# Metaformer block on one core: padded copies laid out by halves of rows, and half A's attention sums taken out of PSUM by ACT and added by Pool

## The reference

```
x = x + conv(layernorm(x))          # over the last axis
t = tokens(x)                       # (16, 1024, 32)
t = t + ffn(layernorm(t))

conv: q, k, v = Wq x, Wk x, Wv x    # 32 x 32 matrices over channels
  qk[n,i,h,j]  = sum_c q[n,c,i,j] k[n,c,h,j] / d
  qrq, krk     = sum_c q[n,c,i,j] rq[c,h,i] / d, the same with k and rk
  weight = softmax over j of (qk + Gq qrq + Gk krk)
  out[n,c,i,j] = sum_h weight[n,i,h,j] Gv1 v[n,c,h,j] + sum_h weight[n,i,h,j] Gv2 rv[c,h,i]
ffn: Wx = t W^T, batch-normed over all tokens, times gamma plus beta
  y_t = sigmoid(Wx_t + y_(t-1) V^T), y_0 = 0
```

## Time and profile before

| | us |
|---|---|
| median of 3 runs | 149.83 (149.29 to 151.29) |
| the profiled execution's own time | 149.44 |
| its span, first to last instruction | 147.7 |
| PE busy | 113.8 (77%) |
| DVE busy | 100.7 (68%) |
| ACT busy | 79.0 (53%) |
| Pool busy | 61.0 (41%) |

### The profile page before, as it was taken

The page is one execution under the profiler, slowest core; times in us unless marked ns, Lnnn a source line. Parts: engine busy times, 40 slices in busy tenths (PEclk is TensorE's granted clock), DMA queues, the critical chain, the costliest instruction groups (busy, mean ns, idle before and its releaser), DMA issues.

```text
span 147.7 us, 4779 instructions
## 1 busy us (share of the span) xinstructions
PE 113.8 (77%) x2102; PEld 80.9 (55%) x2102; DVE 100.7 (68%) x148; ACT 79.0 (53%) x146; POOL 61.0 (41%) x69
## 2 busy tenths in 40 slices
PE   0697995967899999991498598599994987999300
PEld 0322231667887668991498597544331336999300
DVE  5898646060300199789593079999879969788992
ACT  8958767704449997363620003506252459999400
POOL 8995919820000001978820033998052000004940
PEclk9999999999999999999559999999999999999985
DMA  4882640762000000009345200000000000000567
GB/s 142 288 230 37 142 107 0 177 178 83 4 4 4 0 0 4 4 4 208 81 101 129 63 4 7 7 0 0 4 0 0 0 0 0 4 0 0 168 191 209
DMA packets 8287, 9.55 MB, mean 65 GB/s; under 512 B 2316, under 2 KB 6412, under 8 KB 8268
## 3 DMA queue, kind: packets, MB, share of 16 engines
q1 hardware_dynamic: 8268, 9.26, 24.5%
HBM read 2.97 MB, written 2.10 MB: 34 GB/s over the span
## 4 chain that ended last, share of the span: by engine, by line
DVE 28%; PE 28%; ACT 19%; issue 10%; SPq 5%; DMA 4%; POOL 3%; ACTq 0%
PE ps L983 8%; ACT rel_tile L492 6%; PE ps L1019 6%; PE ps L998 5%; ACT warm L634 4%; DVE xin L345 3%; SPq L290 3%; DVE stat L671 3%; DVE u_tile L772 3%; PE ps L1031 3%; DVE y_tile L351 3%; DVE stat L785 3%; DMA xin<-in_x_dram 2%; PE ps L1007 2%; DVE rel_tile L803 2%
## 5 line engine op out<-in xcount | busy, mean ns | idle before, releaser
L401 POOL TENSOR_TENSOR att_tile<-att_tile,soft 128x1024 f32<-128x1024 f32 x4 | 7.8, 1955 | 28.8 <-DVE soft L732 28.8
L492 ACT COPY rel_tile<-ps 128x512 f32<-128x512 f32 x8 | 15.4, 1977 | 4.4 <-PE ps L998 4.3
L571 ACT ACTIVATE square<-y_tile 128x512 f32<-128x512 f32 x8 | 5.1, 640 | 22.6 <-POOL y_tile L422 19.9
L998 PE MATMUL ps<-spread,r_fac 128*32 128x128 f32 x256 | 16.3, 406 | 0.9 <-ACT rel_tile L492 0.7
L351 POOL TENSOR_TENSOR y_tile<-xin,u_tile 128x256 f32<-128x256 f32 (+1 forms) x7 | 7.1, 1048 | 23.5 <-DVE xin L345 23.5
L726 DVE TENSOR_TENSOR att_tile<-ps,rel_tile 128x1024 f32<-128x1024 f32 x4 | 8.3, 2063 | 12.5 <-ACT rel_tile L492 12.5
L1019 PE MATMUL ps<-spread,rv_t 128*32 128x128 f32 x256 | 11.4, 353 | 5.1 <-issue 5.1
L1091 PE MATMUL ps<-blank 128*128 128x512 bf16 x64 | 15.1, 379 | 0.0
L998 PEld LDWEIGHTS ps<-spread,r_fac 128*32 128x32 f32 x256 | 12.3, 126 | 4.5 <-ACT rel_tile L492 3.6
L983 PE MATMUL ps<-spread,u_tile 128*32 128x64 f32 x512 | 12.6, 253 | 2.6 <-issue 1.3
L983 PEld LDWEIGHTS ps<-spread,u_tile 128*32 128x32 f32 x512 | 12.2, 192 | 3.2 <-issue 3.0
(11 more groups left out here) (108 smaller groups left out, 227.2 us busy)
## 6 DMA issues: line engine op xcount, KB each, us to landing
spread<-rel_tile SPq DMA_DIRECT2D x16, 128.0 KB, 2.4
out_dram<-y_tile SPq DMA_DIRECT2D x8, 256.0 KB, 2.3
xin<-in_x_dram SPq DMA_DIRECT2D x3, 512.0 KB, 4.9
spread<-att_tile SPq DMA_DIRECT2D x12, 128.0 KB, 2.4
xin<-in_x_dram SPq DMA_DIRECT2D x2, 256.0 KB, 2.8
spread<-u_tile SPq DMA_DIRECT2D x4, 128.0 KB, 2.3
att_tile<-in_L_conv_rv_dram SPq DMA_DIRECT2D x4, 128.0 KB, 2.5
att_tile<-in_L_conv_rq_dram SPq DMA_DIRECT2D x1, 128.0 KB, 6.1
```

Of the source, the lines that this page charges most:

```text
L492: nc.scalar.copy(rel[:, n // 4, :, rows, :], side_bank(n).rearrange("p (i g j) -> p g i j", i=ROWS, g=G)).then_inc(S["rel_ready"], 1)
L998: ins = nc.tensor.matmul(side_bank(n)[group(q), P * k:P * (k + 1)].rearrange("p (g jp t) -> p g jp t", g=G, t=RUN), r_fac[:, ROWS * n + k, ...
```

## The change

Padded images are stored in halves of rows: `(b jp i t)`, with `b` the half and only 16 rows of pairs in each. The next pair of a row now lies 128 bytes on. The attention weights of half A go to the first 2 KB of each image, and those of half B to the second. `turn_y` on ACT therefore becomes two copies of 512 columns for each `q`, and each `weigh` two instructions, one for each image. The four images `g` of the weights now lie along the first axis of `spread4`, 16 KB apart; before, two were 16 KB apart and two lay 128 bytes apart. Half A's spread waits for `score_a` and the first four relative blocks in place of `score_b_high`. `weigh(1)` moves from Pool to DVE. Half A's weighted sums are copied out of PSUM by ACT (`sums_out`) and added to x2 by Pool (`sums_add`); DVE keeps the row sums. Unit 7's centring and scaling move from DVE to Pool, the last two `bn_part` read PSUM, and the orders are written anew.

```diff
-        y_bd = spread4[:, :, :, :].rearrange("p q g (jp i t) -> p q g jp i t", i=C, t=RUN)
-        att_bd = spread4[:, :, :, :].rearrange("p x q (jp g i t) -> p x q jp g i t", g=2, i=HALF, t=RUN)
+        y_bd = spread4[:, :, :, :].rearrange("p q g (b jp i t) -> p q g b jp i t", b=2, i=HALF, t=RUN)
+        att_bd = spread4[:, :, :, :].rearrange("p g q (b jp i t) -> p g q b jp i t", b=2, i=HALF, t=RUN)
...
             def spread_att(n):
                 wait_weights(sp, n)
-                sp.wait_ge(S["score_b_high"], 1)
+                half, gs = n // 2, slice(2 * (n % 2), 2 * (n % 2) + 2)
+                sp.wait_ge(S["score_b_high" if half else "score_a"], 1)
+                sp.wait_ge(S["rel_product"], PIECES4 // 2 * (half + 1))
                 for q in range(Q):
-                    sp.dma_start(spread4[group(q), n, q, :], rel_tile[group(q), IMG * n:IMG * (n + 1)]
-                                 ).then_inc(S[f"att_in{n // 2}"], 16)
+                    sp.dma_start(spread4[group(q), gs, q, BANK * half:BANK * (half + 1)],
+                                 rel_tile[group(q), IMG * n:IMG * (n + 1)].rearrange("p (g k) -> p g k", g=2)
+                                 ).then_inc(S[f"att_in{half}"], 16)
...
+            def sums_add(k):
+                pool.wait_ge(S["first_sums"], k + 1)
+                nc.gpsimd.tensor_tensor(unit(x2, k), first_sums[:, k, :, :], unit(x2, k), ALU.add).then_inc(S["x2_added"], 1)
...
-                nc.scalar.copy(in_pairs(turned_y[q]), by_pairs(y[:, q, :, :])).then_inc(S["y_turned_act"], 1)
+                for b in range(2):
+                    nc.scalar.copy(in_pairs(turned_y[q])[:, b], by_pairs(y[:, q, HALF * b:HALF * (b + 1), :])).then_inc(S["y_turned_act"], 1)
...
+            def sums_out(k):
+                act.wait_ge(S["wsum_product"], 1)
+                act.wait_ge(S["relv_ready"], 4)
+                nc.scalar.copy(first_sums[:, k, :, :], ps[:, 0:4, :].rearrange("p b (j q i) -> p q i (b j)", q=Q, i=HALF)[:, k]
+                               ).then_inc(S["first_sums"], 1)
...
-                                               r_fac[:, ROWS * n + k, :], y_bd[:, q, :, :, ROWS * n + k, :],
+                                               r_fac[:, ROWS * n + k, :], y_bd[:, q, :, n // 4, :, ROWS * (n % 4) + k, :],
...
-                                               rv_t[:, ROWS * n + k, :], att_bd[:, 2 * half + g // 2, :, :, g % 2, row + k, :],
+                                               rv_t[:, ROWS * n + k, :], att_bd[:, g, :, half, :, row + k, :],
...
-            pe.wait_ge(S["x2_ready"], Q)
-            blank_banks([0, 1] + [WARM_BANK] * 16)
-            for n in range(4):
-                project_wx(n)
-                blank_banks([WARM_BANK] * 4)
-            pe.wait_ge(S["x2_ready"], UNITS)
-            blank_banks([4, 5, 6, 7] + [WARM_BANK] * 10)
+            pe.wait_ge(S["x2_added"], Q)
+            blank_banks([0, 1] + [WARM_BANK] * 8)
+            project_wx(0)
+            blank_banks([WARM_BANK] * 4)
+            project_wx(1)
+            pe.wait_ge(S["x2_ready"], Q)
+            blank_banks([4, 5, 6, 7] + [WARM_BANK] * 6)
+            project_wx(2)
+            blank_banks([WARM_BANK] * 2)
+            project_wx(3)
             project_wx(4)
```

More of the change, by code:

```diff
@@ L167, in recip_of @@
         def recip_of(n):
-            return soft[:, 1, n, :].unsqueeze(2).unsqueeze(3).broadcast_to([P, C, C // RUN, RUN])
+            return soft[:, 1, n // 2, HALF * (n % 2):HALF * (n % 2 + 1)].unsqueeze(2).unsqueeze(3).broadcast_to([P, HALF, C // RUN, RUN])
         def wait_weights(eng, n):
[L171 to L174, removed]
+            eng.wait_ge(S["weights_dve" if n % 2 else "weights"], 2 * (n // 2 + 1))
         def unit(t, k):
@@ L406, in weigh @@
                 pool.wait_ge(S["weight_recip"], n + 1)
-                nc.gpsimd.tensor_tensor(turned_att[:, n, :, :, :], by_pairs(att_m[:, n, :, :]), recip_of(n), ALU.mult
-                                        ).then_inc(S["weights"], 1)
+                for g in range(2):
+                    nc.gpsimd.tensor_tensor(turned_att[:, n, g, :, :, :], by_pairs(att[:, n, g, :, :]), recip_of(2 * n + g), ALU.mult
+                                            ).then_inc(S["weights"], 1)
             shift_scores(0)
@@ L747, in weigh @@
                 dve.wait_ge(S["weight_recip"], n + 1)
-                nc.vector.tensor_tensor(turned_att[:, n, :, :, :], by_pairs(att_m[:, n, :, :]), recip_of(n), ALU.mult
-                                        ).then_inc(S["weights_dve"], 1)
+                for g in range(2):
+                    nc.vector.tensor_tensor(turned_att[:, n, g, :, :, :], by_pairs(att[:, n, g, :, :]), recip_of(2 * n + g), ALU.mult
+                                            ).then_inc(S["weights_dve"], 1)
             score_add(0)
@@ L756, in _ @@
             weight_sum(1)
+            weigh(1)
             score_add(2)
@@ L767, in residual @@
             def residual(k):
[L768 to L771, removed]
+                q = k % Q
+                dve.wait_ge(S["relv_ready"], PIECES4)
+                dve.wait_ge(S["wsum_product"], 2)
+                first = WSUM_BANK[1]
                 nc.vector.tensor_tensor(unit(x2, k),
@@ L774, in residual, with t_sum @@
                                         unit(x2, k), ALU.add).then_inc(S["x2_ready"], 1)
-                dve.wait_ge(S["x2_ready"], k + 1)
-                nc.vector.tensor_reduce(stat2[:, 0, k, :], unit(x2, k), AX_X, ALU.add).then_inc(S["t_sum"], 1)
[L777 to L781, removed]
+            def t_sum(k):
+                if k < Q:
+                    dve.wait_ge(S["x2_added"], k + 1)
+                else:
+                    dve.wait_ge(S["x2_ready"], k + 1 - Q)
+                nc.vector.tensor_reduce(stat2[:, 0, k, :], unit(x2, k), AX_X, ALU.add).then_inc(S["t_sum"], 1)
             def t_sum2(k):
@@ L798, in t_turn @@
             def t_turn(k):
[L799 to L802 removed]
+                dve.wait_ge(S["t_norm"], k + 1)
                 nc.vector.transpose(by_row(tokens, k), unit(x2n, k)).then_inc(S["t_turned"], 1)
             def bn_part(k):
[L806 to L807 removed]
@@ L809, in _ @@
-            residual(0)
+                if k < UNITS - 2:
+                    dve.wait_ge(S["wx_ready"], k + 1)
+                    nc.vector.bn_stats(bn[:, k, :], by_row(wx_q, k)).then_inc(S["bn_part"], 1)
+                else:
+                    dve.wait_ge(S["wx_product"], k + 1)
+                    nc.vector.bn_stats(bn[:, k, :], bank(WX_BANK[k % 2])).then_inc(S["bn_part"], 1)
             relv_out(4)
             relv_out(5)
-            residual(1)
+            t_sum(0)
             relv_out(6)
+            t_sum(1)
@@ L828, in _ @@
             t_turn(1)
             residual(6)
+            t_sum2(4)
+            t_sum(6)
+            residual(7)
+            t_rstd(4)
+            t_sum(7)
             t_turn(2)
-            residual(7)
+            t_sum2(5)
             t_turn(3)
-            t_sum2(4)
-            t_sum2(5)
-            t_rstd(4)
+            t_turn(4)
+            t_rstd(5)
+            t_sum2(6)
             bn_part(0)
-            t_sum2(6)
-            t_rstd(5)
+            t_sum2(7)
             bn_part(1)
-            t_sum2(7)
@@ L841, in _ @@
             t_rstd(6)
-            t_turn(4)
+            bn_part(2)
             t_rstd(7)
-            bn_part(2)
             t_turn(5)
+            bn_part(3)
             t_turn(6)
+            bn_part(4)
             t_turn(7)
-            bn_part(3)
-            bn_part(4)
             bn_part(5)
```

80 lines of the change are left out of this document (40 added, 40 removed).

## The result

The changed kernel takes 140.28 us (median of 4 runs, 140.09 to 140.75), the kernel before 149.83 us (149.29 to 151.29). The ratio is 0.9393 with an interval of 0.9345 to 0.944. The profiled execution took 140.75 us (span 139.0 us), 8.7 us less than the 149.44 us of the profiled execution before.

The account below looks back on a forecast made before the run. Making half A's weights, slowed by L998's SBUF reads, was taken as the bound before the sums, DVE after. 149.44 - 8.85 - 2.6 + 0.1 = 138.1 us, forecast 138.0, range 135.5 to 148.0.

Parts of the forecast that it names:

- The likeliest case: Whole kernel: the new layout speeds the relative scores and the second layer norm shortens; 138.0 us, chance 0.42.
- the 8.85 us for half A's weights: Weights' landing before half A's sums: 9.0 us earlier exponential less 0.15 for split weigh(0), from 72.18 to 63.3.
- Relative scores: L998 matmuls: loads from 52 to 39 ns, blocks 1.25 us, ACT copies 0.63 us, exponential at 51.5, 9.0 us earlier.
- the split copies of y: ACT's copies of y: four of 1024 columns become eight of 512; one pair on the path costs 0.1 us more.
- The inference from the rows: SBUF reads: interleaved by low address bits, L998 keeps all reads in one place, L1019 spreads them over two.
- The rule of the Trainium skill: SBUF sharing: PE and ACT never wait, so the layout changes nothing; rival at 147.0 us, chance 0.22.
- PE's wait: PE before half A's sums: still waits 3.0 us for the weights; a halved clock afterwards matters little.
- `weigh(1)` on DVE and the early wait: Half A's spread: both edits worth nothing, as SP reaches chunk 1 later and half B's scores end earlier anyway.
- The cover of half B's weights: Half B's weights before PE needs them: margin shrinks from 2.3 to 1.1 us, a bound if the first stage gained more.
- Second layer norm: End of half B's sums to the aggregate: 18.4 us after DVE's first add, aggregate 2.7 us earlier, 2.6 counted.
- others are freed but the loads stay at 52 ns: Rival in relative scores: ACT and DVE unblocked, L998 still slow and L1019 slow too; 143.6 us, chance 0.15.
- `relative_values` would block as the relative scores did: Rival in L1019: reads 16 KB apart block DVE's relv_out, costing 6.1 us; 153.0 us, chance 0.15.

Follow-up runs that it names:

- e0: The changed kernel run again without edits, to compare with e8 and e9: 139.85 us (139.05 to 141.08).
- e11: The kernel before with 4 empty words (16 bytes) behind each 16 KB part of the padded copies, nothing else: 140.12 us (139.68 to 140.90).
- e3: The kernel before with 32 empty words (128 bytes) behind each 16 KB part of the padded copies, nothing else: 141.75 us, ratio 0.9396.
- e4: The kernel before with 64 empty words (256 bytes) behind each 16 KB part of the padded copies: 150.17 us (147.62 to 150.26).
- e1: The kernel before with only the new layout of the padded copies; order, waits, sums and statistics as before: 143.16 us, ratio 0.9466.
- e9: The changed kernel with weigh(1) put back on Pool: 139.75 us (138.88 to 141.89).
- e8: The changed kernel with half A's spread waiting for all of half B's scores again: 140.89 us (140.09 to 142.60).
- e7: The changed kernel with the old layout and old wait plus 32 empty words (128 bytes) behind each part: 139.69 us, ratio 0.9209.
- e10: Same as e7 but with 8 empty words (32 bytes) behind each 16 KB part: 137.97 us (137.25 to 138.34).
- e2: The changed kernel with the old layout and the old wait for half B's scores: 149.26 us, ratio 0.9842 to the kernel before.
- e6: The kernel before with 8 empty words (32 bytes) behind each 16 KB part of the padded copies: 139.61 us, ratio 0.926.

## Why the prediction was right

The forecast was 138.0 us, the time 140.28 us: inside the range of 135.5 to 148.0, but just outside the 136.5 to 140 that the forecast had by itself. The gain was 9.55 us where 11.8 were forecast. The likeliest case is the one that came, by its mechanism; too large was one term of its sum, the 8.85 us for half A's weights. One reading was off without an effect on the sum: PE is at 90% or more in 21 of the 40 slices before, not in a third of them.

**Relative scores.** Forecast 39 ns a load and a period of 1.25 us; measured 39.6 ns and copies that start 1.24 us apart. Copies and `score_add` as forecast, 0.60 and 1.23 us. The exponential was put at 51.5 and came at 53.02 in the first trace and at 51.24 in e0's. The difference is the start of the stage, at 42.1 and at 40.9. Over all the traces it lies between 40.5 and 42.5, with old and new layout alike: e11 has the old one and starts latest. So this is scatter of a step that the sum took from one execution. The + 0.1 us for the split copies of y is there, but smaller than this scatter: on the chain the pair takes 1.08 us where the single copy took 1.00.

**The inference from the rows** held in its main point, by e3 and e4: low address bits decide, L998 kept all its reads in one place, and this, not a shared port of DVE and GpSimd, blocked ACT. The rule of the Trainium skill that PE and ACT never wait on anyone ("SBUF — State Buffer", "Who interferes with whom") would have given 147.0 us; e1 with 143.16 us, and e3, which changes addresses alone, speak against it. The two places that I named were too narrow a picture. In it there must be at least four within 256 bytes, of which the new layout uses two, in step.

**Half A's weights.** The mechanism was right, the size was off: the start of the sums moved by 5.9 us in the first trace (7.6 in e0's) where 8.85 were forecast. In e0's trace the stage starts as before and the exponential is where it should be, so what is missing there, 1.3 us, lies behind it: from the first issue of the weights to the sums it took 6.8 us before (65.35 to 72.18) and 8.4 us in e0 (56.20 to 64.62), 8.3 in the first trace. I had taken this stretch to be unchanged. SP's eight issues of half A, before and then after:

```profile
65.35 4.97 SPq L296 DMA_DIRECT2D spread<-rel_tile  x8
```

```profile
58.02 6.45 SPq L297 DMA_DIRECT2D spread<-rel_tile  x8
```

These 1.5 us are the whole difference; the last issue lands 1.8 us after its end in both. Most of it is one issue of 1.80 us, the third (three issues from 59.40 take 3.13 us in the timeline above). The view of all 16:

```profile
L297 SPq DMA_DIRECT2D spread<-rel_tile x16: 585/597/1801, 58.0 to 73.9; - x16
...
DMA to landing us min/median/max: 2.3/2.6/3.9
```

The 15th takes 1.44 us. Before, only the 15th was long, 2.04 us, and hurt nobody. The DMA queues show what goes with a long issue. From 59.2 to 59.7 us, where the third issue starts, the changed kernel has a transfer on the queue that the profile calls instruction, one of 16 such transfers of 16 KB in the span:

```profile
q8 instruction: 1, 0.02, 18.4%
```

The kernel before has none from 64.5 to 73.2 us, around its first eight issues and through PE's wait; there this queue has no row:

```profile
q1 hardware_dynamic: 384, 1.05, 54.2%
```

In all 14 traces together 26 issues of the weights take over 1 us, and each starts within 0.7 us of such a transfer, 25 of them within 0.25 us. So the earlier issues of half A lie beside a transfer that the later ones had missed. This goes by the times alone: no experiment moved the transfers, and why an issue is long beside one stays open.

**PE's wait** was to be 3.0 us and was 3.65. The clock is halved after it as before:

```profile
66.30:69.00 2.70, 2.68 (x52) 2.70 (x56) 1.84 (x4) 2.05 (x2) 2.08 (x2) 0.50 0.03 6
```

That this changes nothing against the kernel before held: from their start to their end half A's sums took 12.6 us, before 13.1. The reason that I gave, that half B's weights come next, didn't: they have landed 2.4 us before PE needs them, and the end of half A's sums is on the chain.

**`weigh(1)` on DVE and the early wait** were to be worth nothing: e9 says so of the first (139.75 against 139.85), e8 of the second within what can be measured. The cover of half B's weights was enough, 2.4 us where 1.1 were forecast: PE goes from half A's sums to L1042 without a wait, at 78.65.

**Sums.** `relative_values` of half B took 41.6 ns a load in place of 35.5, 0.8 us more, which I had left at the old value. This is the change's own cost: it takes L1019 from streams split over two places to streams in step, and e7, with the old layout, has 35.4 ns. But half B's sums are no longer on the chain, so it costs nothing at the end.

**Second layer norm.** Forecast 2.6 us, measured 2.9 by the traces, and 2.1 us by the medians of e3 and e7, which differ only in this part and the order of the weights. Pool's adds took 1.34 us, nearer to the upper bound of 1.43 than to the 1.15 that I took:

```profile
L422 POOL TENSOR_TENSOR u_tile<-att_tile,u_tile 128x512 f32<-128x512 f32 x4 | 5.3, 1340 | 11.1 <-ACT att_tile L580 11.1
```

This delays DVE's first residual of half B to 1.2 us after the sums end (forecast 0.8 us, and within 1 us among the signs). From there to the aggregate it took 17.8 us where 18.4 were forecast. What I had not said plainly: Pool now sets the end. Its share of the chain was 3% before and is 19% now:

```profile
DVE 28%; PE 28%; ACT 19%; issue 10%; SPq 5%; DMA 4%; POOL 3%; ACTq 0%
```

In the changed kernel, e0 and e10 the chain runs from the end of half A's sums through Pool's adds; in e7 it reaches Pool through DVE's row sums. The intervals alone don't decide it. From the end of half A's sums to the aggregate it is 30.4 to 31.3 us with the new sums (32.6 in e2, with PE at half clock in this stage), 32.5 to 33.6 with the old ones; from the end of half B's sums 19.0 to 20.0 (21.6 in e2) and 21.3 to 22.3.

**The rivals.** That others are freed but the loads stay at 52 ns (143.6 us) fell with 39.6 ns. That `relative_values` would block as the relative scores did (153.0 us) fell with `relv_out` (L765), which takes 0.69 us in the timeline of the stage above.

## What to carry to other kernels

When an ACT or DVE instruction takes several times its usual duration beside certain matmuls, compare the addresses that the concurrent streams of these matmuls read: arrays whose parts are a large power of two apart, read at a power-of-two step, may all meet in one place. Eight empty words behind each part cost nothing and brought here 11.4 us of 151, more than the rebuilt layout and as much as the whole change. And when work is moved from one engine to another ahead of a joint stage, look whether the stage's end now hangs on that engine's first instruction and no longer on the last of the other. Where DMA issues are moved ahead into a busy stretch, don't take their duration over from a quiet one: eight of them took 1.5 us more here.

## What the hardware showed that I had not expected

- Four concurrent matmuls whose streams read pairs of fp32 at a step of 256 bytes from equal low addresses slowed ACT's 512-column copy from 0.6 to 2.0 us (before, e2, e4) and DVE's 1024-column add from 1.2 to 4.7 us (before and e2) or 6.4 (e4). Offsets between the streams of 128 bytes (e3), 32 bytes (e6) and 16 bytes (e11) ended it, one of 256 bytes didn't (e4).
- The pace of the loads: 52 ns with equal addresses (before), 36 with offsets of 128 bytes (e3), 28 to 30 with 32 and 16 bytes (e6, e11); a step of 128 bytes with all streams in step gave 37 to 42 ns (the changed kernel, e0).
- A Pool add of two full 512-column inputs took 1.34 us, though the centring of the same width with one full input takes 1.05 us.
- One to three of SP's 16 issues of the weights take 1.1 to 2.1 us where the others take 0.6 us, each within 0.7 us of a 16 KB transfer on the queue that the profile calls instruction.
